# Gated attention and expert block on one core: the loads of x for batches two and later move from SyncE's queue to ScalarE's

## The reference, cut to what matters

```
x: (8, 512, 2048)   ctx: (8, 512, 2048)          # batch, feature, position
z   = layernorm(x, axis=-1)                      # over the 2048 positions of a row
q, k = Wq z + bq, Wk z + bk ; v = Wv ctx + bv    # in windows of 128 positions
att = softmax(q.k / sqrt(32))                    # 8 heads, window by window
o   = gelu(att v)
x   = x + tanh(g_x) * (Wo o + bo) * mask
w   = top-8 of softmax(layernorm(x) Wr + rb)     # 64 experts, per row of x
x   = x + tanh(g_f) * (layernorm(x) * sum(w) + w @ expert_bias)
```

## Time and profile before

| | us |
|---|---|
| runs | 1185.96, 1180.27, 1179.55 (median 1180.27) |
| the profiled execution, whole | 1178.47 |
| its span, first to last instruction | 1176.7 |
| PE busy | 1122.1 (95%) |
| PEld busy | 1041.6 (89%) |
| ACT busy | 1028.7 (87%) |
| DVE busy | 947.1 (80%) |
| POOL busy | 719.8 (61%) |

### The profile page before, as it was taken

The page is one execution under the profiler, slowest core; times in us unless marked ns, Lnnn a source line. Parts: engine busy times, 40 slices in busy tenths (PEclk is TensorE's granted clock), DMA queues, the critical chain, the costliest instruction groups (busy, mean ns, idle before and its releaser), DMA issues.

```text
span 1176.7 us, 32708 instructions
## 1 busy us (share of the span) xinstructions
PE 1122.1 (95%) x11661; PEld 1041.6 (89%) x11661; DVE 947.1 (80%) x1833; ACT 1028.7 (87%) x3200; POOL 719.8 (61%) x684
## 2 busy tenths in 40 slices
PE   2899999999999999999999999999999999999976
PEld 2798999899998999899998999989999899989965
DVE  6868878988789977889778887889778997787767
ACT  3798989989999899988999989999899989999954
POOL 2675767467655667566764676747765667655621
PEclk9899999999999999999999999999999999999989
DMA  9468454786547954588456765478554785556433
GB/s 289 110 171 216 112 136 114 249 208 156 135 121 257 229 133 121 151 249 210 125 132 215 210 178 134 122 248 234 128 131 124 254 230 135 127 173 172 112 83 144
DMA packets 160162, 199.39 MB, mean 169 GB/s; under 512 B 26496, under 2 KB 102272, under 8 KB 159872
## 3 DMA queue, kind: packets, MB, share of 16 engines
q1 hardware_dynamic: 158848, 196.80, 61.2%
q10 hardware_dynamic: 1152, 0.50, 0.2%
HBM read 79.67 MB, written 33.65 MB: 96 GB/s over the span
## 4 chain that ended last, share of the span: by engine, by line
PE 63%; DVE 11%; SPq 7%; ACT 7%; issue 4%; POOL 3%; DMA 3%; ACTq 0%; DVEq 0%; POOLq 0%
PE ring L308 8%; PE ring L310 7%; PE ring L309 7%; SPq L519 7%; PE ring L365 4%; PE ring L348 4%; ACT T L616 4%; PE ring L384 4%; PE ring L386 4%; PE ring L385 4%; PE ring L323 3%; PE ring L325 3%; PE ring L324 3%; PE ring L403 3%; PE ring L453 2%
## 5 line engine op out<-in xcount | busy, mean ns | idle before, releaser
L616 ACT ACTIVATE T<-ring,nmx 128x128 f32<-128x128 f32 x1024 | 359.6, 407 | 29.9 <-DVE nmx L772 28.9
L308 PE MATMUL ring<-z_hi,wqk_hi 128*128 128x256 f32 x1024 | 298.4, 291 | 26.0 <-DVE z_lo L954 21.8
L310 PE MATMUL ring<-z_lo,wqk_hi 128*128 128x256 f32 x1024 | 291.3, 284 | 0.0
L309 PE MATMUL ring<-z_hi,wqk_lo 128*128 128x256 f32 x1024 | 291.1, 284 | 0.0
L616 ACT ACTIVATION_READ_ACCUMULATOR T<-ring,nmx 128x1 f32 x1024 | 252.2, 247 | 0.0
L1044 POOL TENSOR_TENSOR z_lo<-z,z_hi 128x1024 fp32r<-128x1024 f32 x62 | 147.7, 2382 | 161.9 <-ACT z_hi L584 161.9
L308 PEld LDWEIGHTS ring<-z_hi,wqk_hi 128*128 128x128 f32 x1024 | 197.1, 193 | 38.6 <-DVE wqk_lo L930 21.8
L778 DVE STREAM_TRANSPOSE T<-T 128x512 f32<-128x512 f32 x256 | 169.8, 691 | 45.2 <-ACT T L616 44.8
L1056 POOL TENSOR_TENSOR X<-X,xt 128x512 f32<-128x512 f32 x128 | 165.8, 1295 | 56.3 <-DVE xt L805 56.1
L310 PEld LDWEIGHTS ring<-z_lo,wqk_hi 128*128 128x128 f32 x1024 | 197.6, 193 | 0.0
L309 PEld LDWEIGHTS ring<-z_hi,wqk_lo 128*128 128x128 f32 x1024 | 197.4, 193 | 0.0
(11 more groups left out here) (134 smaller groups left out, 2672.2 us busy)
## 6 DMA issues: line engine op xcount, KB each, us to landing
PT<-T SPq DMA_DIRECT2D x1018, 80.0 KB, 2.2
X<-in_x SPq DMA_DIRECT2D x64, 512.0 KB, 5.6
cx<-in_ctx SPq DMA_DIRECT2D x128, 256.0 KB, 3.9
out_y<-X SPq DMA_DIRECT2D x128, 256.0 KB, 3.1
mg<-in_mask SPq DMA_DIRECT2D x64, 128.0 KB, 3.6
sel<-rows_d SPq DMA_DIRECT2D x128, 3.0 KB
X<-in_eb SPq DMA_DIRECT2D x2, 512.0 KB, 8.6
X<-in_wqT SPq DMA_DIRECT2D x1, 512.0 KB, 4.8
```

The lines of the kernel that those rows point to most:

```text
L308: e.matmul(o, wqk_hi[:, t, cols], z_hi[:, t, :], t == 0, False)
L309: e.matmul(o, wqk_lo[:, t, cols], z_hi[:, t, :], False, False)
L310: last = e.matmul(o, wqk_hi[:, t, cols], z_lo[:, t, :], False, t == DT - 1)
L616: last = e.activation(T[u % 2][:, :, n, :], bank("S", 4 * u + g)[:, k * W:(k + 1) * W].rearrange("p (b j) -> p b j", b=4), ACT.Exp, bias=n ...
```

## The change

The eight loads of each of batches 2 to 7, 48 in all, are issued by ScalarE instead of SP, with the same two waits for the stores of batch b - 2. Their slots change from 50.75 in steps of 5 to 61 in steps of 4. Batch 1's loads and all stores, moves, ctx, mask and small loads stay on SP.

```
-    sx=44.75, sx_gap=1.25, x2=45.25, rl=50.75, rl_gap=5,
+    sx=44.75, sx_gap=1.25, x2=45.25, rl=61, rl_gap=4,
...
 @block.sync
-            def load_x(b, t, h):
-                if b >= 2:
-                    e.wait_ge(out_done[t][2 * h], out_value(b - 2))
-                    e.wait_ge(out_done[t][2 * h + 1], out_value(b - 2))
-                e.dma_start(X[b % 2][:, t, h * 1024:(h + 1) * 1024],
-                            xv[b, t, :, h * 1024:(h + 1) * 1024]).then_inc(x_in[t][h], 16)
+            def load_x(t, h):
+                e.dma_start(X[1][:, t, h * 1024:(h + 1) * 1024],
+                            xv[1, t, :, h * 1024:(h + 1) * 1024]).then_inc(x_in[t][h], 16)
...
-                for i in range(8):
-                    for b in batch(t, C["rl"] + C["rl_gap"] * i):
-                        if b + 2 < NB:
-                            load_x(b + 2, i // 2, i % 2)
...
 @block.scalar
+            def load_x(b, t, h):
+                e.wait_ge(out_done[t][2 * h], out_value(b - 2))
+                e.wait_ge(out_done[t][2 * h + 1], out_value(b - 2))
+                e.dma_start(X[b % 2][:, t, h * 1024:(h + 1) * 1024],
+                            xv[b, t, :, h * 1024:(h + 1) * 1024]).then_inc(x_in[t][h], 16)
...
+                for i in range(8):
+                    for b in batch(t, C["rl"] + C["rl_gap"] * i):
+                        if b + 2 < NB:
+                            load_x(b + 2, i // 2, i % 2)
```

More of the change, by code:

```diff
@@ L573, in _ @@
                         e.wait_ge(v_m, V_SW)
-                    load_x(1, i // 2, i % 2)
+                    load_x(i // 2, i % 2)
             for t in range(DT):
```

## The result

| | before | after |
|---|---|---|
| median of the runs, us | 1180.23 (4 runs) | 1196.73 (4 runs, 1194.22 to 1198.79) |
| profiled execution / its span, us | 1178.47 / 1176.7 | 1198.79 / 1196.9 |
| mean granted clock of TensorE | 0.993 | 0.987 |

The ratio is 1.0132, 95% interval 1.0100 to 1.0165: 16.5 us slower. The forecast was 1184 with a range up to 1196; the direction was right, the size (3.7 us on the same scale) was over four times too small. The median lies 0.7 us above the range's end, and by the ratio, 1.0132 of the 1180.27 that the forecast started from, the time is 1195.8, just inside it. The profile is of the slowest of the four executions; the two fastest, 1194.22 and 1194.97, had a mean granted clock of 0.991.

A forecast was written before the change was run, and what follows sets the result against it. TensorE was taken as the bound, busy 139.25 of 141 us a batch. 1178.5 + 5.4 (later loads) - 0.6 (SP) + 0 (ScalarE) = 1183.3, up to 1.8 more on the runs' median: forecast 1184, range 1176 to 1196.

The forecast's parts named there:

- Taken off SP: SP's queue: eight fewer issues a batch and no x data ahead of moves; -0.6 us, ends 0 and -3.9.
- Later loads: VectorE's statistics of x: load 3 lands after 5.4 us, wanted after 4.5; 0.9 us in 6 batches, 5.4 us.
- Put on ScalarE: ScalarE's eight issues a batch: cost taken as 0, with 0.64 us an issue as the other end.
- Rival C: ScalarE pays for the issues, say 2 us a batch, 12 us: 1190.5; chance 0.10.
- Rival A: Loads amid moves are slow: load 3 needs 8.9 us, VectorE waits 4.4 us each batch, 26 us: 1205; chance 0.18.
- Rival B: Relief of SP's queue reaches TensorE: all 3.9 us of waits in batches 1 and later vanish, 1174.6; chance 0.12.
- What would show it: Signs in the profile: VectorE's x waits of 0.9 us, about six; moves landing near 2.5; TensorE's PT waits about 9.

The follow-up runs named there:

- the small loads: The changed kernel with each of the 48 x loads cut to 64 columns in place of 1024, issues and places kept: 1175.81 us, 0.9956.
- the old slots on ScalarE: The changed kernel with its x loads on ScalarE's queue at slots 50.75 in steps of 5: 1214.24 us, 1.0282.
- three groups on SP's queue: The kernel before with its x loads on SP in groups of two, three and three, placed between the moves: 1181.04 us, 1.0008.
- the same groups on ScalarE's: The changed kernel with its x loads on ScalarE in groups of two, three and three, behind a unit's 16 exponentials: 1192.45 us, 1.0105.
- among the moves: The kernel before with its x loads on SP's queue among a unit's 16 moves, at the changed kernel's places in time: 1211.66 us, 1.0239.

## Why the prediction went wrong, in its path and so in its size

*Taken off SP: this step failed.* It said that without x data ahead of them the moves land after some 2.5 us in place of 4, and priced the relief at -0.6 us, its ends at 0 and -3.9. Nothing on the other side of zero was allowed for. The x data did not go away: it went into another queue and into the moves' own time. The moves of the unit with loads 3 to 5 land after 6.0 us, TensorE waits 13.9 us more, and 7.5 us of halved clock follow. The earlier trace rows had it before my eyes, 4.2 us against 2.1 with x in flight; I read them as the cost of standing behind x in one queue and not of sharing with x, and rows 11 (8.9 us for a load with moves about) only as a danger to x, not to the moves. The sentence of the Trainium skill that I drew on (DMA: Bandwidth & Descriptors, Issuing engines are not separate DMA queues) said that the copies interleave on the same engines. The trace agrees (79.6% of the time for ScalarE's queue beside 20.5% for SP's), and I drew too little from it: less than no gain was possible.

*The clock was not priced at all.* I had the level 1.00 in the window of a batch and no wait in front of L365 over 1.6 us in the whole run; the changed kernel has waits from 1.9 us on, and five were followed by 3.41 us at half speed.

*Later loads: right in kind, too large.* Forecast 5.4 us in six waits of 0.9 at load 3; measured 2.8 us in four, of which the longest was 1.17; two of the four are at load 1, which was said to have 6 us or more and landed after 8.4 and 7.9 us in those batches. Load 3 went out 2.3 us into the moves, where 1.5 was said (388.4 less 387.05 is 1.35). The landing median of the 48 loads is 6.1, where 5.4 was taken:

```profile
DMA to landing us min/median/max: 3.7/6.1/9.5
```

That the landings are longer and the waits shorter than forecast may be because VectorE was itself later, as TensorE had waited before; no run shows it by itself. The wait in the fourth unit behind the stores, which should have grown by 0.9 each, is 1.8 us in the six batches together, before 2.8: the path from late x over VectorE and GpSimd to TensorE, which carried the whole forecast, cost nothing that can be seen.

*Put on ScalarE: right.* Zero, though an issue costs 0.33 us of sequencer time. Rival C is refuted by the small loads.

*Rival A* gave a number near the measured one for part of its range, but its mechanism is refuted by the old slots on ScalarE, where x is in time and the loss doubles. That the measured time lies at the very end of the range and not far outside it is luck: that end was drawn for A and C, and neither is what happened. *Rival B* failed: the waits left over in the fourth unit stay with no x data at all.

*What would show it* named signs that tell: the waits in the second and third unit behind the stores were to be gone, and that of the second grew from 1.2 to 8.5 us over the six batches, with 7.6 us new in the first (the third had 0.1 before and after); the moves were to land after 2.5, and landed after 6.0. For this outcome, moves later than before, the prediction had no sign and no rival.

## What to carry to other kernels

When a transfer moves to a second queue, ask what it overtakes. In one queue the program's order was a schedule for the DMA engines: bulk loads written between bursts of small copies stayed out of their way (1.0008 with three groups on SP's queue), and a second queue, issued when another engine came to it, gave that order up (1.0105 with the same groups on ScalarE's). A poor place costs in one queue too (1.0239 among the moves). Price it with the landing time of the small copies beside the bulk data against that without it, both of which the trace before may hold, and add what TensorE's clock loses behind a wait.

## What was not expected of the hardware

A wait of TensorE of 1.89 to 2.55 us was followed by one stretch of 3.41 us at a granted clock of 0.50 in five cases; one of 5.43 us went with 6.8 us. The relation is not strict: with half as large copies, waits of 2.0 and 2.5 us were followed by none, nor was the one of 2.50 us shown above, nor one of 3.50 us with the old slots on ScalarE. Two queues at work did not share the DMA engines by halves: three loads on one left the moves on the other a fifth of the time, with rows of 4 KB and of 2 KB alike. The same program on ScalarE's queue with loads between the moves took 1183.5 to 1200.5 us in ten runs, while its twin on SP's queue took 1177.0 to 1184.2.
